# First loads on swapped queues, a split last scatter, and the third attention's weights loaded into spent expert memory, in a four-layer transformer kernel

## The reference

```
x += attn(LN(x), ctx, ctx; tau, delta)    # 16 heads of 16, 128 keys, L0
x += routed(LN(x)) + shared(LN(x))        # 8 experts, each takes its 512 best tokens, L0
x += attn(LN(x), ctx, ctx; tau, delta)    # L1
x += bitlinear FFN(LN(x))                 # L1
x += windowed attention(ctx, LN(x))       # L2
x += product-key experts(LN(x))           # L2: 8 heads choose 8 of 4096 rows of down and up
x += attn(LN(x), ctx, ctx; tau, delta)    # L3
x += top-2 of 8 experts(LN(x))            # L3

attn(q, k, v) = softmax((qWq+bq)(kWk+bk)^T * tau + delta, scaled) (vWv+bv) Wo + bo
```

## Time and profile before

| | |
|---|---|
| runs | 3211.59, 3206.2, 3208.53 us; median 3208.53 us |
| profiled execution | 3210.37 us; span of its instructions 3208.6 us |
| mean granted TensorE clock | 0.977 |
| busy share of the span | PE 95%, PEld 72%, DVE 73%, ACT 34%, POOL 30% |

### The profile page before, as it was taken

How to read it: one execution, slowest core, us unless ns; L and a number is a source line. 1 busy time by engine, 2 the same in 40 slices (tenths; PEclk the granted TensorE clock), 3 DMA queues, 4 the chain that set the end, 5 groups by cost and what they waited for, 6 DMA issues and landing times. The chain is left out here.

```text
span 3208.6 us, 63608 instructions
## 1 busy us (share of the span) xinstructions
PE 3057.4 (95%) x25734; PEld 2297.1 (72%) x25750; DVE 2338.5 (73%) x6169; ACT 1093.6 (34%) x1915; POOL 973.1 (30%) x1065
## 2 busy tenths in 40 slices
PE   8998999999899989888999999999999977998999
PEld 6777766566677756677888888888888865777444
DVE  6888355111488889666999899989998965888666
ACT  4554221222356679443222222222222204554000
POOL 3433000233343322002444444444444443332000
PEclk9999999999999999999999999999999978999999
DMA  4000220243401000411000000000000002000000
GB/s 149 28 28 2 76 76 20 71 116 96 130 28 41 2 11 1 145 39 64 5 4 6 5 4 4 6 4 5 4 6 4 5 3 94 28 28 2 14 20 20
DMA packets 82691, 112.23 MB, mean 35 GB/s; under 512 B 12256, under 2 KB 62688, under 8 KB 82016
## 3 DMA queue, kind: packets, MB, share of 16 engines
q1 hardware_dynamic: 72784, 97.25, 9.1%
q0 software_dynamic: 6144, 8.52, 1.4%
q10 hardware_dynamic: 3472, 2.37, 0.2%
HBM read 87.02 MB, written 21.10 MB: 34 GB/s over the span
## 5 line engine op out<-in xcount | busy, mean ns | idle before, releaser
L2129 POOL TENSOR_TENSOR pk_hisig<-pk_hihot,pk_sigs 128x512 f16<-128x512 f16 x512 | 520.5, 1044 | 665.9 <-DVE pk_hihot L2404 664.5
L2227 PE MATMUL pk_ps<-X,ew_downT 128*128 128x256 f32 x2048 | 481.1, 386 | 0.0
L2273 PE MATMUL pk_ps<-ew_up,pk_act_h 128*128 128x256 f32 x2048 | 461.4, 384 | 1.7 <-DVE pk_act_h L2392 1.7
L2273 PEld LDWEIGHTS pk_ps<-ew_up,pk_act_h 128*128 128x128 f32 x2048 | 390.4, 192 | 57.7 <-issue 2.0
L2227 PEld LDWEIGHTS pk_ps<-X,ew_downT 128*128 128x128 f32 x2048 | 381.4, 191 | 60.3 <-issue 14.8
L2137 ACT ACTIVATE pk_act_h<-pk_ps 128x512 f32<-128x512 f32 x256 | 152.9, 598 | 546.0 <-PE pk_ps L2227 545.9
L2405 DVE TENSOR_TENSOR pk_lohot<-pk_iota_h,pk_ps 128x1024 f16<-128x1024 f16 x256 | 311.2, 1216 | 0.0
L635 DVE TENSOR_REDUCE a_mx<-a_ps_s 128x8 f32<-128x1024 f32 x192 | 225.3, 1216 | 20.4 <-PE a_ps_s L494 20.3
L2606 PE MATMUL mo_ps<-mw_we,mo_xnT 128*128 128x512 f32 x512 | 225.8, 598 | 0.0
L640 DVE TENSOR_TENSOR a_probs<-a_ps_s,a_mx 128x1024 f32<-128x1024 f32 x192 | 225.3, 1215 | 0.0
L2392 DVE TENSOR_TENSOR pk_act_h<-pk_act_h,pk_ps 128x512 f32<-128x512 f32 x256 | 171.9, 682 | 61.0 <-PE pk_ps L2257 61.0
(11 more groups left out here) (355 smaller groups left out, 5281.7 us busy)
## 6 DMA issues: line engine op xcount, KB each, us to landing
ro_w<-in_L_W SPq DMA_DIRECT2D x16, 1024.0 KB, 7.5
i_ctx_t<-in_ctxT SPq DMA_DIRECT2D x24, 512.0 KB, 3.9
i_tau<-in_tau SPq DMA_DIRECT2D x24, 256.0 KB, 4.2
i_delta<-in_delta SPq DMA_DIRECT2D x24, 256.0 KB, 5.0
X<-in_x SPq DMA_DIRECT2D x4, 1024.0 KB, 13.5
row_dram<-sh_row SPq DMA_DIRECT2D x8, 512.0 KB, 3.0
sum_dram<-sh_new SPq DMA_DIRECT2D x8, 512.0 KB, 3.3
X<-sum_dram SPq DMA_DIRECT2D x4, 1024.0 KB, 9.2
```

The lines of the kernel that those rows point to most:

```text
L2129: ins = pool.tensor_tensor(hisig[:, buf, n, :, :, :], hi, sig2.broadcast_to([P, TP, 2, ECH]), ALU.mult)
L2227: ins = pe.matmul(hid.bank(f"h{c}")[:, j * 2 * P:(j + 1) * 2 * P], downT[:, k, e * P:(e + 1) * P], XT[:, p, k, :], start=(k == 0), stop=(k ...
L2273: ins = pe.matmul(tail.bank("y")[:, 0:D], act_h[:, p % 2, c, s * P:(s + 1) * P], up[:, c, :], start=(c == 0), stop=(c == ECH - 1))
```

## The change

Five edits:

1. First attention: SP issues the weights first and then the inputs and quarters 1 to 3 of `X`; ACT issues quarter 0. Before, SP issued quarter 0, the inputs and the other quarters, ACT the weights. The first spin goes from 16 to 26.
2. All attentions: values (0,0) stand ahead of tile 0's scores in PE's queue.
3. Routed stage, last expert: each chunk is scaled and scattered by itself; only the last of the four scatters is left for the second attention. The second spin of the second attention goes from 56 to 36.
4. `experts_w` becomes two sets, `down_w` and `up_w`, loaded in the same order. `downT` is kept through the third attention.
5. The third attention's weights and first inputs (11 DMAs, `late`) are loaded by SP at the end of its product-key queue, when PE has run the last `hidden`, into the rows of `downT`. The third attention issues no loads of its own weights and inputs, and its spin of 20 is gone.

```diff
+class Within(Ahead):
+    def place(self, name, row, shape):
...
+        part = self.rows[row][:, self.used[row]:self.used[row] + size]
...
 # attention, sync
-            if arrival:
-                arrival.load(sp, 0)
             if load_first:
+                w.load(sp)
                 inputs.load(sp)
             if arrival:
-                for q in range(1, 4):
+                for q in range(1 if arrival.x_first else 0, 4):
                     arrival.load(sp, q)
             load(1)
             following.load(sp)
 # attention, scalar
-            if load_first:
-                w.load(act)
+            if arrival and arrival.x_first:
+                arrival.load(act, 0)
 # attention, tensor
+            values(0, 0, ps_o[:, :])
             pe.wait_ge(zero_ready, 4)
             scores(0, 0, 0)
-            values(0, 0, ps_o[:, :])
 # routed_ffn, gpsimd
+                    else:
+                        for c in range(SLOTS - 1):
+                            pool.wait_ge(y_ready, e + 2 + c)
+                            scatter_rows(pool, got, y, sum_dram, s, range(c, c + 1))
 # routed_ffn, vector
+                    if e == EXPERTS - 1:
+                        dve.wait_ge(scores_out, e + 2)
+                        for u in range(SLOTS):
+                            main.wait_full(dve, e, f"y{u}")
+                            main.take(dve.tensor_tensor(tmp[:, u, :], main.bank(f"y{u}")[:, 0:D], b2[:, s, :], ALU.add),
+                                      f"y{u}")
+                            main.wait_taken(dve, e, f"y{u}")
+                            dve.tensor_scalar(y[:, s, u, :], tmp[:, u, :], score[:, s, u:u + 1], None,
+                                              ALU.mult).then_inc(y_ready, 1)
+                        break
 # windowed_attention, sync
+            first_following.load(sp)
             following.load(sp)
 # product_key_experts, sync, behind the loads of xo
+            hid.wait_full(sp, PAIRS - 1, f"h{UNITS - 1}")
+            late.load(sp)
 # product_key_experts, tensor
-            experts_w.wait(pe)
+            down_w.wait(pe)
+            up_w.wait(pe)
 # build
-                  arrival=Arrival(x_loaded, load_inputs, x_first=True), spins=(16, 0))
+                  arrival=Arrival(x_loaded, load_inputs, x_first=True), spins=(26, 0))
-            scatter_rows(pool, got, y, sum_dram, 1)
+            scatter_rows(pool, got, y, sum_dram, 1, range(SLOTS - 1, SLOTS))
-                  arrival=Arrival(sums_loaded, load_sums, scatter=scatter_last), spins=(0, 56))
+                  arrival=Arrival(sums_loaded, load_sums, scatter=scatter_last), spins=(0, 36))
+        late = Within(nc, "a3", [down_w.at["downT"][:, k, :] for k in range(KC)])
...
-        experts_w.free()
-        att_w = attention_weights(3)
+        up_w.free()
-        att_in = attention_inputs(3, "left")
-        attention(nc, keep, "a3", att_w, att_in, a["ctxT"], moe_w, load_first=True, spins=(20, 0))
+        attention(nc, keep, "a3", late, late, a["ctxT"], moe_w)
```

More of the change, by code:

```diff
@@ L156, in is_last, with __init__ @@
     return isinstance(g, int) and g == GROUPS - 1
+class Within(Ahead):
+    def __init__(self, nc, tag, rows):
+        self.stack, self.rows = ExitStack(), rows
+        self.loaded = nc.alloc_semaphore(f"{tag}_w_loaded")
+        self.at, self.sources, self.used = {}, [], [0] * len(rows)
+    def place(self, name, row, shape):
+        size = 1
+        for n in shape:
+            size *= n
+        part = self.rows[row][:, self.used[row]:self.used[row] + size]
+        self.used[row] += size
+        names = "abc"[:len(shape)]
+        if len(shape) > 1:
+            part = part.rearrange("p (%s) -> p %s" % (" ".join(names), " ".join(names)),
+                                  **dict(zip(names[1:], shape[1:])))
+        self.at[name] = part
+        return part
 def ready_root(act, keep):
@@ L848, in gather_rows, with scatter_rows @@
                                 ).then_inc(got["gathered"][s], 16)
-def scatter_rows(pool, got, y, sum_dram, s):
-    for c in range(SLOTS):
+def scatter_rows(pool, got, y, sum_dram, s, chunks=range(SLOTS)):
+    for c in chunks:
         pool.indirect_dma_start(out=sum_dram[:, :], in_=y[:, s, c, :], in_offset=None,
@@ L1682, with windowed_attention @@
 MASKED = 1e9
-def windowed_attention(nc, keep, w, ctxT, following):
+def windowed_attention(nc, keep, w, ctxT, first_following, following):
     tag = "wa"
@@ L2006, with product_key_experts @@
 UNITS = ECH // 2
-def product_key_experts(nc, keep, w, experts_w, x_dram):
+def product_key_experts(nc, keep, w, down_w, up_w, late, x_dram):
     tag = "pk"
@@ L2020, in product_key_experts @@
         XT = X[:, :, :].rearrange("p (a u) d -> p a (u d)", u=2).rearrange("p a (k n) -> p a k n", k=KC)
-        downT, up = experts_w.at["downT"], experts_w.at["up"]
+        downT, up = down_w.at["downT"], up_w.at["up"]
         wm = sb("wm", [P, KC, 2 * PK_HEADS * PK_KEYS])
@@ L2752, in build @@
         with ExitStack() as c2:
-            id_zero = c2.enter_context(nc.semaphore("id_zero"))
+            id_zero = semaphore("id_zero")
             block = c2.enter_context(nc.Block())
@@ L2818, in build @@
         att_in.free()
-        experts_w = Ahead(nc, "ew", "right", [
-            ("downT", [P, KC, PK_EXPERTS], F32, chunked(a["L2_downT"][:, 0:PK_EXPERTS])),
+        down_w = Ahead(nc, "dw", "right", [
+            ("downT", [P, KC, PK_EXPERTS], F32, chunked(a["L2_downT"][:, 0:PK_EXPERTS]))])
+        up_w = Ahead(nc, "ew", "right", [
             ("up", [P, ECH, D], F32, a["L2_up"][0:PK_EXPERTS, :].rearrange("(c p) n -> p c n", p=P))])
-        windowed_attention(nc, keep, win_w, a["ctxT"], experts_w)
+        windowed_attention(nc, keep, win_w, a["ctxT"], down_w, up_w)
         win_w.free()
@@ L2826, in build @@
         x_dram = nc.dram_tensor("x_dram", (P, TILES * D), F32, kind="Internal").ap()
+        late = Within(nc, "a3", [down_w.at["downT"][:, k, :] for k in range(KC)])
+        w3 = {k: a[f"L3_{k}"] for k in ("wq", "wk", "wv", "wo", "bq", "bk", "bv", "bo")}
+        for m in ("wk", "wv", "wq", "wo"):
+            late.add(late.place(m, 0, (KC, D)), chunked(w3[m]))
+        for m in ("bq", "bk", "bv"):
+            late.add(late.place(m, 0, (KC,)), w3[m])
+        late.add(late.place("bo", 0, (D,)), w3["bo"])
+        late.add(late.place("ctx_t", 1, (2, KC, GT))[:, 0, :, :], chunked(a["ctxT"])[:, :, 0:GT])
+        for m in ("tau", "delta"):
+            late.add(late.place(m, 1, (2, GT))[:, 0, :], a[m][:, 0:GT])
         product_key_experts(nc, keep, {
             "wq": a["L2_w_q"].rearrange("(c p) n -> p c n", p=P), "keys": a["L2_keys"], "gamma": a["L2_gamma"],
-            "beta": a["L2_beta"]}, experts_w, x_dram)
-        experts_w.free()
-        att_w = attention_weights(3)
+            "beta": a["L2_beta"]}, down_w, up_w, late, x_dram)
+        up_w.free()
         moe_w = Ahead(nc, "mw", "right", [("gate", [P, KC, P // G], F32, chunked(a["L3_gate"])),
                                  ("we", [P, KC, MOE, D], F32, a["L3_we"])])
-        att_in = attention_inputs(3, "left")
-        attention(nc, keep, "a3", att_w, att_in, a["ctxT"], moe_w, load_first=True, spins=(20, 0))
-        att_in.free()
-        att_w.free()
+        attention(nc, keep, "a3", late, late, a["ctxT"], moe_w)
         top2_experts(nc, keep, moe_w, out)
```

## The result

The changed kernel takes 3179.1 us (median; 3176.45 to 3180.38, 4 runs), beside 3207.36 us (3201.98 to 3211.59, 4 runs) for the kernel before: ratio 0.9905, 95% interval 0.9893 to 0.9917. Its profiled execution took 3180.38 us with a span of 3178.6 us and a mean granted clock of 0.979, where before had 3210.37, 3208.6 and 0.977. The forecast was 3176.6, its range 3170 to 3187.

What follows compares the result with a forecast made beforehand. The prediction took PE, busy 95% of the span, as the bound. Gains of 5.3, 7.6 and 19.0 us in the three attentions sum to 31.9, giving 3178.5 profiled and a forecast median of 3176.6 us, range 3170 to 3187.

Steps and rivals of the forecast that it cites:

- What bounds the kernel: Whole kernel: PE, busy for 95% of the span; a start that comes earlier is worth its length at the end.
- First attention: First attention's start: 2.6 us from the order of loads and 2.7 from values first, together 5.3 us.
- Rival B: First loads: the swapped queues give nothing, as the same 16 engines carry both; 29.3 us gained, 3179.2; chance 0.09.
- Late loads: Third attention's loads ahead of time: cost nothing, keys start with the stage, queries and all behind them 16.2 us earlier.
- rival C: Third attention: late loads don't run ahead, SP being held until the stage's end; 8.9 us less, 3185.5; chance 0.04.
- Third attention: Third attention's start: loads ahead of time and values ahead of scores together gain 19.0 us, the queries' clock staying.
- rival A: Shortened starts: the clock falls in the third attention, costing 5 us, 3181.7; second too, 3184 to 3186; chance 0.18.
- Last scatter split: Second attention's start: block ends 0.7 us earlier, last scatter lands earlier, reload and columns come 6.6 us earlier.
- Values first in the second attention: Second attention: values (0,0) ahead of tile 0's scores gain 1.0 us, `norm(1)` being the next late thing.
- D: All attentions: tile rate, not start, sets each end, the gain is waited away; within 0.2% of 3208.5; chance 0.03.
- E: Third attention: without its spin it stays at the low clock, so the kernel is slower, 3217; chance 0.02.

Runs made afterwards that it cites:

- e8: The changed kernel with quarter 1 of `X` put between the weights and the inputs in SP's queue: 3184.15 us, one execution.
- e4: The changed kernel with tile 0's scores ahead of values (0,0) again in all three attentions: 3185.53 us.
- e1: The changed kernel with two early scatters instead of three, the last two issued in the second attention: 3181.18 us, one execution.
- e2: The changed kernel with POOL waiting at the routed block's end for the landing of the three early scatters: 3181.39 us, one execution.
- e7: The changed kernel with all four scatters in the second attention again, scaling still chunk by chunk, spin 56: 3181.91 us, one execution.
- e9: The changed kernel with all four scatters and the first quarter's reload of `X` in the routed block, second attention's spin 4: 3170.54 us.
- the filler: The changed kernel with five matmuls on the identity between bias row and columns of the third attention: 3178.98 us.

## Why the prediction held, and where its terms were off

- **What bounds the kernel**: right. What was won at the starts was found at the stages' ends (stage table).
- **First attention** (5.3, measured 5.65): right. Rival B falls: undoing the swap costs 2.3 of the 2.6 us, and in e8, within one queue, the order alone moves the keys by 3.2. The keys' low clock (6.24 us) came as assumed; the spin ended at 9.63, not 10.9.
- **Late loads** (nothing waits, keys with the stage): right; rival C falls with 2563.28. The first softmax moved by 16.1 us (forecast 16.0), the second by 18.2. That the first fits so well is luck: the queries began 17.3 us earlier, not 16.2, and then took 1.5 us longer than at the held clock.
- **Third attention** (19.0, measured 17.8): the step that assumed the clock to stay in the queries failed in this profile; held, it would be 20.5 (71.88 - 51.4). This is rival A in part, with 2.6 instead of 5 us.
- **Last scatter split** (6.6 with the earlier scaling): the mis-sized term, 2.7 measured (0.67 + 2.05). The scaling did end 0.7 us earlier; the step "so the block ends 0.7 earlier" failed, because POOL's own end of the block, its `DRAIN`, came 3.2 us after the point that the scaling would have set. The working has POOL "nothing else" to do behind the early scatters and puts this at nothing. The trace of before shows the `DRAIN` of 4.62 us in the same block, but 13 us ahead of the block's end, where it cost nothing; the rows that were read don't include it.
- **Values first in the second attention** (1.0): worth 1.5 by e4, given back to the clock at tile 1's scores in the profiled execution, and to a fall somewhere in this start in eight of the eleven profiles with this order. In the third attention (3.0 of its 19.0) the second fall, at tile 1's scores, left little of it.
- **The total**: 30.0 us of the forecast 31.9, of which 3.7 lie in stretches for which no gain was forecast. The forecast time is thus nearer than its terms, by luck; the changed starts alone gave 26.3, and with them alone the time would have been some 3182, still inside the range.
- D and E fall with the stage table. The clock fell for some microseconds and came back each time.

What stays open is why POOL's `DRAIN` takes 4.6 to 5.0 us behind the scatters, whether the filler in the third attention keeps the clock up, and whether edits 4 and 5 shortened the windowed attention and the product keys.

## What to carry to other kernels

When work is moved to the end of a stage, ask what that engine's own end of the stage costs, not only what the data wait for. Look for its closing instruction in the trace, also where other engines' work still hides it: the view by source line shows it, the timeline doesn't. If such a hold can't be avoided, put the next transfers ahead of it, so that it runs beside them. A stall of PE that becomes shorter is not yet a gain if nothing keeps the clock up in what is left of it; compare two profiles of the same kernel before a difference of 2 us is given a cause.

## What the runs showed of the hardware

- POOL's `DRAIN` at the end of a block took 4.6 to 5.0 us behind indirect scatter-adds (before, the changed kernel, e1, e2, e7, e9), also when these had landed (e2: 4.87; e7 and before: 4.62); it ended 2.0 us behind indirect gathers and 0.1 us behind plain work (before). Where it ended last, the next stage's keys began 0.4 us later, 5.3 to 5.5 us after POOL had nothing left to do.
- The same program's clock falls at different places: the second attention's queries took 3.70 us and tile 1's scores 1.92 in one profile of the changed kernel, 5.40 and 1.06 in the other. The Trainium skill, TensorE: Matmul & The Clock Gate, Part 1, says that the point varies from run to run; the two profiles agree, and so do 51.4 and 54.0 us for the third attention's start, whose code is the same in the kernels that have one or the other.
